# K of the first batch by quarters, h of the last tile by quarters, the context's low part on VectorE

## The reference

```python
def attn(x, cond, mask):                       # x: layernorm of the input, 16 heads of 32
    q = w8a8_linear(x, wq, bq)                 # rows of x and of wq rounded to int8 levels
    k = cond @ wk.T + bk                       # float32, no rounding
    v = cond @ wv.T + bv
    scores = einsum('bhnd,bhld->bhnl', q, k) / sqrt(32) + mask
    o = einsum('bhnl,bhld->bhnd', softmax(scores), v)
    return w8a8_linear(o, wo, bo)
x = x + attn(layernorm(x), ctx, mask)
def ffn(x):                                    # x: layernorm again
    h = gelu(quant(x) @ quant(W1).T * scales + B1)     # 2048 columns
    return quant(h) @ quant(W2).T * scales + B2        # every row of h has its own scale
x = x + ffn(layernorm(x))
```

## Time and profile before

| | us |
|---|---|
| median of 3 runs | 663.83 (659.75 to 665.29) |
| the profiled execution, whole | 658.58 |
| its span in the trace | 656.4 |
| outside the span | 2.2 |

### The profile page before, as it was taken

One profiled execution on the slowest core, in us unless ns is written; L12 is line 12 of the kernel. 1 busy time (PEld: TensorE's weight loads), 2 busy tenths in 40 slices (PEclk: granted clock), 3 DMA queues, 4 the chain that ended last, 5 costly groups with the idle time before them and its releaser, 6 DMA issues.

```text
span 656.4 us, 15000 instructions
## 1 busy us (share of the span) xinstructions
PE 638.5 (97%) x5204; PEld 470.9 (72%) x5204; DVE 474.1 (72%) x1175; ACT 461.1 (70%) x1156; POOL 223.6 (34%) x455
## 2 busy tenths in 40 slices
PE   8898999999999999999999989999999999999999
PEld 4667787777777777768777777877777786767534
DVE  4989788767676766876775834775688768777874
ACT  3545676777887667787687867786777778879702
POOL 3343343252527153530525243341444252321100
DMA  9965865523252443413214253217145231413020
GB/s 313 248 193 143 274 115 175 118 45 80 53 116 61 61 87 61 96 37 79 76 40 85 64 73 40 64 50 124 26 94 60 74 70 27 51 36 74 9 49 33
DMA packets 80586, 58.68 MB, mean 89 GB/s; under 512 B 57984, under 2 KB 67968, under 8 KB 79872
## 3 DMA queue, kind: packets, MB, share of 16 engines
...
## 4 chain that ended last, share of the span: by engine, by line
PE 75%; DVE 11%; DMA 5%; issue 4%; POOL 3%; ACT 2%; ACTq 0%; DVEq 0%; SPq 0%; POOLq 0%
PE ps_ring L1070 32%; PE ps_t L1104 12%; PE ps_s L1097 7%; PE ps_ring L1176 7%; PE ps_t L1116 6%; PE ps_ring L1189 6%; PE ps_ring L1138 2%; PE ps_ring L1063 1%; DMA w_q<-in_w1T 1%; PE ps_s L1165 1%; DVE cols L843 1%; PE ps_ring L1126 1%; DMA yqT<-o_q 1%; DMA x_in<-in_x 1%; DVE probs L872 1%
## 5 line engine op out<-in xcount | busy, mean ns | idle before, releaser
L872 DVE CUSTOM_DVE_ANT_0 probs<-ps_s,mask_in 112x375 f32<-112x375 f32 x256 | 129.6, 544 | 67.8 <-PE ps_s L1097 54.9
L690 ACT ACTIVATE probs<-probs,neg_max 112x375 f32<-112x375 f32 x256 | 154.5, 607 | 27.1 <-DVE neg_max L872 24.6
L700 ACT ACTIVATE pT<-ps_t 125x336 f32<-125x336 f32 x256 | 109.8, 446 | 70.6 <-PE ps_t L1104 64.7
L1104 PEld LDWEIGHTS ps_t<-ident,probs 112*125 112x125 f32 x768 | 107.9, 188 | 42.3 <-issue 18.6
L1104 PE MATMUL ps_t<-ident,probs 112*125 112x112 f32 x768 | 119.9, 278 | 5.6 <-ACT oT L707 2.4
L609 POOL TENSOR_TENSOR ctx_lo<-ctx_in,ctx_hi 128x376 fp32r<-128x376 f32 x60 | 63.8, 1071 | 124.7 <-ACT ctx_hi L668 124.6
L1070 PE MATMUL ps_ring<-ctx_hi,wk_hi 128*128 128x376 f32 x256 | 90.7, 354 | 1.2 <-DVE wk_lo L765 0.7
L1070 PE MATMUL ps_ring<-ctx_hi,wk_lo 128*128 128x376 f32 x256 | 85.5, 334 | 0.0
L1070 PE MATMUL ps_ring<-ctx_lo,wk_hi 128*128 128x376 f32 x256 | 85.4, 334 | 0.0
L1070 PE MATMUL ps_ring<-wv_hi,ctx_hi 128*125 128x512 f32 x192 | 79.1, 412 | 2.0 <-DVE o L882 1.0
L1070 PE MATMUL ps_ring<-wv_lo,ctx_hi 128*125 128x512 f32 x192 | 75.8, 395 | 0.0
...
## 6 DMA issues: line engine op xcount, KB each, us to landing
...
h<-in_w2T SPq DMA_DIRECT2D x4, 1024.0 KB, 5.9
b_row<-in_w2T SPq DMA_DIRECT2D x4, 1024.0 KB, 6.8
...
xres<-in_x ACTq DMA_DIRECT2D x14, 256.0 KB, 2.6
out<-y ACTq DMA_DIRECT2D x14, 256.0 KB, 2.0
...
w_q<-in_w1T SPq DMA_DIRECT2D x2, 1024.0 KB, 11.3
```

The source lines that it names most:

```text
L690: nc.scalar.activation(probs[:, hd % SP_RING, :], probs[:, hd % SP_RING, :], ACT.Exp, scale=-1.0, bias=neg_max[:, b % 2, hd:hd + 1], accum ...
L700: nc.scalar.activation(pT[0:LR, hd % PT_RING, :], att_bank("T", b, hd)[0:LR, 0:LC * N], ACT.Copy).then_inc(pT_s, 1)
L872: nc.vector.tensor_tensor_reduce(out=probs[:, hd % SP_RING, :], in0=ps_s[hd % HG][0:N, 0:L], in1=mask_in[:, b % 2, :], scale=-1.0, scalar= ...
L1104: last = nc.tensor.transpose(bank[0:LR, lc * N:(lc + 1) * N], probs[:, hd % SP_RING, lc * LR:(lc + 1) * LR], ident[0:N, 0:N])
```

## The change

1. K of batch 0 (`k0`, `k_first`): the loop over the four slices of the contraction is outermost and the four K units are inside, so that slice k needs only `ctx_lo` of slices up to k and the half of `wk_lo` that holds it. The four results lie in `ps_s`; ACT reads them from there. The warm products of the start go to `ps_t`.
2. h of the last tile: DVE rounds the quarters 0, 1 and 2 (512 columns each), ACT quarter 3. PE transposes each into a bank of its own outside the ring, in the order 0, 3, 1, 2, DVE copies out 0 and 2, ACT 3 and 1, and `down` takes the quarters in that order, each as soon as it is there.
3. `ctx_lo` of the batches 1 to 15 is DVE's.
4. All five lists are written anew. 7 warm units go: 2 at the start (after the change 12 stand in a row ahead of K instead of 9), and the 5 behind the last `down`. ACT loads x ahead of the context; SP loads wq between the halves of wk, and the bias rows after W1.

```diff
-            def split_lo(b, i):
-                if b == 1 and i == 0:
-                    pool.wait_ge(ctx_lo_s, 4)
-                pool.wait_ge(ctx_hi_s, 4 * b + i + 1)
-                wait_for(pool, k_pe, 4 * (b - 1))
-                wait_for(pool, v_pe, 3 * (b - 1))
-                nc.gpsimd.tensor_tensor(ctx_lo[:, b % 2, i, :], ctx_in[:, i, :], ctx_hi[:, b % 2, i, :].bitcast(FP32),
-                                        ALU.subtract).then_inc(ctx_lo_s, 1)
...
             def split_lo(b, i):
-                dve.wait_ge(ctx_hi_s, i + 1)
-                nc.vector.tensor_tensor(ctx_lo[:, 0, i, :], ctx_in[:, i, :], ctx_hi[:, 0, i, :].bitcast(FP32), ALU.subtract
+                dve.wait_ge(ctx_hi_s, 4 * b + i + 1)
+                wait_for(dve, k_pe, 4 * (b - 1))
+                wait_for(dve, v_pe, 3 * (b - 1))
+                nc.vector.tensor_tensor(ctx_lo[:, b % 2, i, :], ctx_in[:, i, :], ctx_hi[:, b % 2, i, :].bitcast(FP32), ALU.subtract
                                         ).then_inc(ctx_lo_s, 1)
...
+            def k_first(b, k):
+
+                pe.wait_ge(w_lo, k // 2 + 1)
+                pe.wait_ge(ctx_lo_s, k + 1)
+                for g in range(KC):
+                    cols = slice(g * P, (g + 1) * P)
+                    for t, (w, c) in enumerate(((wk_hi, ctx_hi), (wk_hi, ctx_lo), (wk_lo, ctx_hi))):
+                        last = nc.tensor.matmul(ps_s[g][:, 0:LP], w[:, k, cols], c[:, 0, k, :],
+                                                start=(k == 0 and t == 0), stop=(k == KC - 1 and t == 2))
+                    if k == KC - 1:
+                        last.then_inc(k_pe, 1)
...
+            def h_quarter(j):
+                part = slice(j * C, (j + 1) * C)
+                nc.vector.tensor_scalar(h[:, part], h[:, part], h_r, ROUND, ALU.mult, ALU.add).then_inc(h_round_lo, 1)
+                dve.wait_ge(h_round_lo, LAST + 1 + j)
+                nc.vector.tensor_scalar(h_q[:, part], h[:, part], -ROUND, None, ALU.add).then_inc(h_quant_lo, 1)
...
+                if t == LAST:
+                    act.wait_ge(down_pe, t)
+                    for bank, j, count in ((ps_s[2], 3, 4), (ps_s[3], 1, 5)):
+                        act.wait_ge(last_T, count)
+                        nc.scalar.activation(hT[:, 4 * j:4 * j + 4, :].rearrange("p k n -> p (k n)"), bank[:, 0:C // 2].bitcast(BF16), ACT.Copy
+                                             ).then_inc(hT_act, 1)
...
             def down(b, i):
+                quarter = i
+                if b == LAST:
+                    quarter = (0, 3, 1, 2)[i]
+                    pe.wait_ge(*((hT_dve, 1), (hT_act, 1), (hT_act, 2), (hT_dve, 2))[i])
```

More of the change, by code:

```diff
@@ new lines @@
+xs_in 1.0 load_row 0.1 x_T 1.0 prepare 0.10 0.12 load_row 0.2 prepare 1.0 1.1 xs_out 2.0 prepare 1.2 r_move 0.0 x_T 2.0 xs_in 2.0
+prepare 1.3 1.6 r_move 1.0 prepare 1.8 xs_out 3.0 o_T 0.0 prepare 1.10 x_T 3.0 xs_in 3.0 prepare 1.12 y_T 0.0 r_move 2.0 x_T 4.0
+xs_out 4.0 h_T 0.0 0.1 o_T 1.0 xs_in 4.0 y_T 1.0 xs_out 5.0 r_move 3.0 xs_in 5.0 o_T 2.0 h_T 1.0 1.1 y_T 2.0 x_T 5.0 r_move 4.0
+o_T 3.0 xs_out 6.0 h_T 2.0 xs_in 6.0 x_T 6.0 h_T 2.1 y_T 3.0 xs_out 7.0 r_move 5.0 h_T 3.0 o_T 4.0 xs_in 7.0 x_T 7.0 h_T 3.1 y_T
@@ L50 @@
+11.0 x_T 15.0 xs_out 15.0 xs_in 15.0 y_T 11.0 r_move 14.0 h_T 11.0 o_T 12.0 h_T 11.1 y_T 12.0 r_move 15.0 h_T 12.0 12.1
 """
 POOL_UNITS = """
-x_norm 0.0 x_quant 0.0 split 1.0 1.1 1.2 x_norm 1.0 split 1.3 q 0.0 split 2.0 x_quant 1.0 split 2.1 2.2 2.3 q 1.0 x_norm 2.0 split
-3.0 3.1 x_quant 2.0 residual 0.0 split 3.2 x_norm 3.0 split 3.3 q 2.0 x_quant 3.0 split 4.0 y_norm 0.0 x_norm 4.0 split 4.1 q 3.0
-split 4.2 4.3 y_quant 0.0 x_quant 4.0 residual 1.0 split 5.0 y_norm 1.0 x_norm 5.0 split 5.1 q 4.0 residual 2.0 split 5.2 5.3
@@ L115 @@
[L115 to L118 removed]
+x_load 0.0 ctx_load 0.0 0.1 split 0.0 0.1 w_hi 0.0 split 0.2 0.3 w_hi 0.1 ctx_load 1.0 w_hi 0.2 0.3 ctx_load 1.1 x_load 1.0 split
@@ L154 @@
-13.3 h_absmax 13.1 13.2 13.3 h_quant 13.0 h_T 13.0 13.1 down 13.3
+x_norm 0.0 split 0.0 0.1 x_quant 0.0 w_lo 0.0 w_rows 0.0 split 0.2 w_rows 0.1 w_lo 0.1 0.2 w_rows 0.2 split 0.3 w_lo 0.3 w_rows
+0.3 0.4 prepare 0.0 w_rows 0.5 split 1.0 q 0.0 split 1.1 prepare 0.1 split 1.2 1.3 x_norm 1.0 prepare 0.2 S 0.0 0.1 0.2 x_quant
+1.0 prepare 0.3 0.4 S 0.3 w_max 0.0 split 2.0 prepare 0.5 split 2.1 prepare 0.6 0.7 S 0.4 prepare 0.8 0.9 S 0.5 prepare 0.10 S 0.6
+0.7 prepare 0.11 x_norm 2.0 S 0.8 prepare 0.12 S 0.9 0.10 0.11 split 2.2 q 1.0 split 2.3 prepare 1.0 S 0.12 0.13 0.14 0.15 prepare
@@ L155 @@
+15.15 down 11.3 up 12.0 12.1 12.2 h_absmax 12.0 up 12.3 h_absmax 12.1 12.2 12.3 h_quant 12.0 gather 13.0 o_quant 13.0 o_T 13.0
+out_proj 13.0 y_norm 13.0 y_quant 13.0 down 12.3 y_T 13.0 up 13.0 13.1 h_absmax 13.0 13.1 up 13.2 13.3 h_absmax 13.2 13.3 h_quant
+13.0 h_T 13.0 13.1 down 13.3
 """
 PE_UNITS = """
-warm 0.0 0.1 0.2 0.3 0.4 0.5 0.6 0.7 0.8 k 0.0 warm 0.9 k 0.1 0.2 0.3 warm 0.10 w_T 0.0 0.1 warm 0.11 w_T 0.2 warm 0.12 w_T 0.3 v
-0.0 0.1 q 0.0 v 0.2 warm 0.13 w_T 0.4 0.5 warm 0.14 v 1.0 w_T 0.6 S 0.0 w_T 0.7 v 1.1 w_max 0.0 T 0.0 0.1 w_max 0.1 S 0.1 v 1.2 T
@@ L191 @@
-15.11 15.12 up 12.0 12.1 12.2 12.3 PV 15.2 T 15.13 warm 1.0 T 15.14 15.15 warm 1.1 PV 15.3 warm 1.2 gather 13.0 warm 1.3 1.4 1.5
-1.6 o_T 13.0 out_proj 13.0 warm 1.7 1.8 1.9 down 12.0 warm 1.10 down 12.1 12.2 12.3 y_T 13.0 warm 1.11 up 13.0 13.1 13.2 13.3 warm
-1.12 1.13 1.14 1.15 1.16 1.17 h_T 13.0 13.1 warm 1.18 down 13.0 13.1 13.2 13.3 warm 1.19 1.20 1.21 1.22 1.23
+warm 0.0 0.1 0.2 0.3 0.4 0.5 0.6 0.7 0.8 0.9 0.10 0.11 k0 0.0 0.1 0.2 w_T 0.0 0.1 k0 0.3 v 0.0 w_T 0.2 0.3 warm 0.12 q 0.0 v 0.1
@@ L194 @@
+11.1 T 15.8 15.9 S 15.3 down 11.2 T 15.10 down 11.3 PV 15.1 T 15.11 15.12 up 12.0 12.1 T 15.13 up 12.2 12.3 warm 1.0 T 15.14 warm
+1.1 T 15.15 PV 15.2 15.3 warm 1.2 gather 13.0 warm 1.3 1.4 1.5 1.6 o_T 13.0 warm 1.7 out_proj 13.0 warm 1.8 1.9 down 12.0 12.1
+12.2 warm 1.10 down 12.3 warm 1.11 y_T 13.0 warm 1.12 up 13.0 13.1 13.2 13.3 warm 1.13 1.14 1.15 1.16 1.17 1.18 h_T 13.0 down 13.0
+13.1 h_T 13.1 down 13.2 13.3
 """
@@ L220 @@
 RING_USES = [use for use in turns(PE_UNITS)
-             if use[0] in ("w_T", "so", "w_max", "q", "k", "v", "gather", "o_T", "out_proj", "y_T", "up", "h_T") or use[0] == "down" and use[2] == 0]
+             if use[0] in ("w_T", "so", "w_max", "q", "k", "v", "gather", "o_T", "out_proj", "y_T", "up") or use[0] == "down" and use[2] == 0]
 RING_AT = {use: n for n, use in enumerate(RING_USES)}
```

339 lines of the change are left out of this document (178 added, 161 removed).

## The result

| | before | after |
|---|---|---|
| median of 20 runs each, us | 660.35 (658.45 to 665.29) | 667.55 (662.57 to 671.99) |
| ratio | | 1.0106, 95% interval 1.0082 to 1.0130 |
| profiled execution, us | 658.58 | 665.5 |
| its span, us | 656.4 | 663.7 |

What follows compares the result with a forecast made beforehand. PE was taken to bound the middle, DVE the start, chains the ends. Terms -2.1 - 3.5 + 1.0 + 1.0 - 2.0 sum to -5.6 us: 653.0 profiled, 658.2 as median, 0.85% below 663.83; range 648 to 667.

Steps and rivals of the forecast that it cites:

- The end: Last tile to the span's end: three parts, (a), (b) and (c), sum to -2.1 us, range -3.0 to -1.3.
- (a): Span's end: without the warm products behind the last `down`, it ends some 0.35 us behind the store's landing: -1.4 us.
- (b): Last tile, h by quarters: `down` ends at 650.66 in place of 651.62, -1.0 us.
- (c): Last tile: a warm unit now stands between `o_T` and `out_proj`, +0.3 us on the chain.
- The start: Up to the end of batch 0: x's scales earlier, first `T` near 45.1 against 47.28; -3.5 us, bounds 0 and -6.
- The +1.0 given back until 120: After batch 0 until 120 us: busy DVE gets 12 more splits, 6.5 us, giving back 1.0 us.
- DVE's added load in the middle: 120 to 600 us: sixty splits on DVE sometimes delay a maximum by 0.5 us; +1.0 us (0 to +5).
- Rival 1: DVE's relief is real work won: start gives -6, middle -4, -12 in all, 651.8 us; chance 0.33.
- The hole at 391 gone: Middle: PE's idling at 391 us for a late `ctx_lo` from POOL disappears; -2.0 us (0 to -2.3).
- The lists written anew: Middle: new lists can close or open holes anywhere; 0, from -5 to +5 us.
- Rivals 2 to 4: 2: start gives nothing, 662.7, chance 0.09; 3: DVE becomes the bound, 677, 0.07; 4: splits hold POOL's chains, 665, 0.09.
- Rival 4: POOL's y chains are held by DVE's splits, +7, 665 us; lists worse by themselves look alike, +5; chance 0.09.

Runs made afterwards that it cites:

- e1: The change's code (K and h by quarters, last five warm units gone) under the lists of before, low part on POOL: 658.63 us, 1.0023 of before.
- e3: The change with its own lists, the 60 low-part subtractions given back to POOL where DVE had run them: 670.01 us, 1.0187 of before.
- e13: The change with the scales written through a row of SBUF and the low part back on POOL: 655.83 us, 0.9955 of before.
- e10: The change with each write of the scales made in two, through a row of SBUF, then to DRAM: 647.49 us, 0.9824 of before.
- e12: Before, with only the write of the scales made in two, through a row of SBUF: 655.18 us, 0.9939 of before.
- e2: e1 with the 60 low-part subtractions moved to DVE, each ahead of the masking that followed POOL's in time: 680.93 us, 1.0349 of before.
- e7: The change without the writes of x's row scales to DRAM from batch 2 on (stale rows used): 647.69 us, 0.9832 of before.
- e8: Before without the writes of x's row scales to DRAM from batch 2 on (stale rows used): 656.25 us, 0.9970 of before.
- e9: The change with all scale writes kept, but from batch 2 on the read takes stale rows and waits for no write: 655.08 us, 0.9961 of before.

## Why the prediction was wrong, step by step

- **The end** (-2.1): right. Gather to end 34.2 to 32.2 us. (a) The store is issued at 661.17 and the span ends 2.5 us later (2.4 forecast). (b) From the first transposes of h (655.53) to the end of the last product (658.46 + 1.89) 4.8 us (4.64 forecast) against 5.8 before (646.02 to 648.16 + 3.63). (c) `out_proj` 0.38 us later (0.3). e1 shows that (b) needs `h_T 13.1` behind two quarters of `down`.
- **The start** (-3.5): right in number, the first K product at 14.08 (14.0 forecast), the first `T` at 45.22 (45.1); but the path to it was wrong, and that the number fits is luck. `xs_in` went out at 23.62, `xs_bc` landed at 30.2 and not at 34, and DVE's `q` ran at 31.35. `w_T 0.4`, which was to wait for just that at 34.1, did start at 34.00, but behind PE's own V products and without a wait (the row has no bracket):

```profile
33.76 0.40 PE L1090 MATMUL ps_ring<-wv_hi,ctx_lo 128*125 128x512 f32 x1
34.00 0.40 PE L1054 MATMUL ps_ring<-ident_bf,h_q 128*128 128x128 bf16 x4
```

  The +1.0 given back until 120 did not come by 107 (3.9 us kept); at 115.61 then came the hole of 4.16 us.
- **DVE's added load in the middle** (+1.0; DVE near 497 us, measured 491.5): not borne out, and not refuted by itself. Against POOL at the same places of the new lists the low part on DVE is worth -0.8% with the slow writes (e3) and -1.3%, 8 us, without them (e13 to e10); but with the write out of the way the middle of the change takes what the middle of before takes (e10 and e12), so the +1.0 does not show either. Rival 1, DVE's relief, had 651.8 or 1.8% below before; beside before by a row the change is 1.15% below, nearer to the forecast's 0.85% than to that. e2 shows the other side: a subtraction in the wrong place on DVE costs microseconds, not 0.54.
- **The hole at 391 gone** (-2.0): it went, and another came next to it. Up to 396.99 PE idles 2.03 us for DVE's multiplication by `xs_bc`, whose scales were written from 384.50 and read only from 391.99. What is late next was not asked there.
- **The lists written anew** (0, from -5 to +5): **this step failed.** The middle lost 13.3 us where it was to lose 5 at most. The reason given for the bound was that PE's holes in the trace of before hold 6.4 us, and by the same measure 5 could be lost; but holes that are not there yet have no such bound. I had before me SP's new list, in which `h_T 2.0`, `r_move 5.0`, `h_T 3.0`, `h_T 6.1` and `h_T 7.1` stand right behind an `xs_out`, and the trace of before, in which the write takes 7 us and the context loads issued behind one 7.1 against 3.5; I took SP's list as an order without prices. e7 and e8 show the price, 2.7% in the new lists and 0.3% in the old; e9 splits it: half of it SP's standing at the read, half the late landings.
- **Rivals 2 to 4**: the start did give its gain, and DVE did not become the bound. Rival 4's mechanism is in the trace, but small. The links of POOL's chain for y, before and after (shortest, median and longest in ns):

```profile
L589 POOL TENSOR_SCALAR y_nw<-y_rs,y_nw x39: 343/344/347, 122.0 to 605.8; 128x1 f32<-128x1 f32 x39
...
L591 POOL TENSOR_SCALAR y_nw<-y_rs,y_nw x39: 343/344/1461, 121.4 to 615.5; 128x1 f32<-128x1 f32 x39
```

  Some links take 1 us and more with the splits on DVE: the 13 chains take 3.5 us in the median where they took 3.2, and 46.9 us in all where they took 41.5; in e10, the fastest kernel, they take as long (46.7). Rival 4 had "lists that are worse by themselves" at 665, close to what came, but without a mechanism, and its chance (0.09 for both halves) was low for what came. Of the three signs named beforehand, one came true: PE's idling from 120 to 600 grew beyond 10 us, to 14.2.
- **The range** (648 to 667): 667.55 lies just above it. The chance of slower by over 1% was 0.08. The forecast stood on a median of three runs, 663.83; over 20 runs before is at 660.35, and 0.85% below that is 654.7, so the miss is 1.9% in ratio, more than the distance from 658.2 says.
